# Factorization machine on one core: the remainders of V are computed on GpSimd instead of VectorE

## The reference

```python
B, VOCAB, F = (512, 6250, 64)
xf = x.astype(V.dtype)                      # x: int32, 0 or 1
xv = xf @ V                                 # V: 6250 x 64 float32
sum_sq = jnp.sum(xv * xv, axis=-1)
sq_sum = xf @ jnp.sum(V * V, axis=-1)
second_order = 0.5 * (sum_sq - sq_sum)
linear = g_bias + xf @ bias
return linear + second_order[:, None]       # 512 x 1
```

## Time and profile before

| | before |
|---|---|
| time, median of 3 runs (lowest, highest) | 48.98 us (48.85, 49.02) |
| profiled execution: its own time | 49.03 us |
| profiled execution: span | 47.2 us |
| mean granted TensorE clock in it | 0.996 of full |
| busy: DVE, PE, POOL, ACT | 30.5, 22.0, 20.5, 13.7 us |

### The profile page before, as it was taken

How to read it: one execution, slowest core, us unless ns; L and a number is a source line. 1 busy time by engine, 2 the same in 40 slices (tenths; PEclk the granted TensorE clock), 3 DMA queues, 4 the chain that set the end, 5 groups by cost and what they waited for, 6 DMA issues and landing times.

```text
span 47.2 us, 634 instructions
## 1 busy us (share of the span) xinstructions
PE 22.0 (46%) x210; PEld 20.1 (43%) x210; DVE 30.5 (65%) x74; ACT 13.7 (29%) x30; POOL 20.5 (43%) x34
## 2 busy tenths in 40 slices
PE   0000000000000000045999995999999999997200
PEld 0000000000000000045989893998999899985100
DVE  2000000000999469997999899999999999998600
ACT  0000009100899469954996300020002000000000
POOL 1999800000199009999599999990000000000000
PEclk9999999999999999999999999999999999999998
DMA  0399999999999999999999999999999970000000
GB/s 0 102 152 100 109 140 152 164 189 158 175 174 172 181 170 178 146 142 108 105 106 106 106 106 106 101 104 103 116 96 101 94 55 3 0 0 0 0 2 0
DMA packets 5583, 4.87 MB, mean 103 GB/s; under 512 B 1434, under 2 KB 5581, under 8 KB 5581
## 3 DMA queue, kind: packets, MB, share of 16 engines
q0 software_dynamic: 3456, 3.21, 73.4%
q1 hardware_dynamic: 1155, 0.82, 6.7%
q10 hardware_dynamic: 970, 0.81, 5.3%
HBM read 14.48 MB, written 0.00 MB: 307 GB/s over the span
## 4 chain that ended last, share of the span: by engine, by line
DVE 42%; DMA 34%; ACTq 10%; issue 4%; PE 2%; ACT 1%
DMA v_in<-in_L_rec_V_dram 34%; DVE x_all L330 13%; DVE seen L344 13%; ACTq L150 5%; DVE v_rest L295 3%; ACTq L237 3%; DVE xv L354 3%; DVE w_sum L301 2%; DVE xv_sq L359 2%; DVE odd_turned L335 2%; PE xv_ps L466 2%; ACTq L233 2%; DVE seen L406 1%; ACTq L234 1%; DVE seen L350 1%
## 5 line engine op out<-in xcount | busy, mean ns | idle before, releaser
L466 PE MATMUL xv_ps<-wall,x_all 128*128 128x195 bf16 x192 | 19.9, 266 | 1.8 <-DVE x_all L330 1.8
L466 PEld LDWEIGHTS xv_ps<-wall,x_all 128*128 128x128 fp8e4 x192 | 18.0, 105 | 2.7 <-DVE x_all L330 1.1
L160 POOL DMA_DIRECT2D x_all<-in_r_x_dram x24 | 13.0, 551 | 0.8 <-POOLq L498 0.8
L216 POOL TENSOR_TENSOR wall<-v_rest 128x512 bf16<-128x512 f32 (+1 forms) x6 | 7.4, 1247 | 10.2 <-DVE v_rest L295 10.2
L450 PE MATMUL g_ps<-g_in,ones 1*128 1x1 f32 x2 | 0.6, 342 | 20.2 <-DMA g_in<-in_L_rec_g_bias_dram 20.2
L450 PEld LDWEIGHTS g_ps<-g_in,ones 1*128 1x128 f32 x2 | 0.5, 305 | 20.2 <-issue 20.2
L330 DVE STREAM_TRANSPOSE x_all<-x_all 128x512 uint32<-128x512 uint32 (+1 forms) x13 | 8.5, 652 | 0.0
L364 DVE MEMSET v_in<- 22x64 f32 x1 | 0.1, 112 | 10.6 <-DMA v_in<-in_L_rec_V_dram 10.6
L344 DVE TENSOR_TENSOR seen<-seen,x_all 128x512 uint32<-128x512 uint32 (+1 forms) x10 | 6.3, 628 | 0.0
L251 ACT ACTIVATE v_sq<-v_in 128x512 f32<-128x512 f32 (+1 forms) x6 | 3.8, 636 | 5.3 <-DVE v_in L364 3.5
L295 DVE TENSOR_TENSOR v_rest<-v_in 128x512 f32<-128x512 f32 (+1 forms) x6 | 4.3, 750 | 1.4 <-DMA v_in<-in_L_rec_V_dram 1.3
(11 more groups left out here) (27 smaller groups left out, 9.5 us busy)
## 6 DMA issues: line engine op xcount, KB each, us to landing
x_all<-in_r_x_dram POOLq DMA_DIRECT2D x12, 196.0 KB, 9.7
v_in<-in_L_rec_V_dram ACTq DMA_DIRECT2D x6, 128.0 KB, 13.3
v_in<-in_L_rec_V_dram SPq DMA_DIRECT2D x6, 128.0 KB, 11.3
x_all<-in_r_x_dram POOLq DMA_DIRECT2D x4, 100.0 KB, 7.4
x_all<-in_r_x_dram POOLq DMA_DIRECT2D x4, 64.0 KB, 8.5
x_all<-in_r_x_dram POOLq DMA_DIRECT2D x4, 32.0 KB, 8.1
bias_in<-in_L_rec_bias_dram ACTq DMA_DIRECT2D x3, 6.5 KB
v_in<-in_L_rec_V_dram SPq DMA_DIRECT2D x1, 24.0 KB
```

What stands on the lines that cost most here:

```text
L160: queue.dma_start(x_words[S * i:S * i + S, t, :, lo // QUAD:hi // QUAD].bitcast(fp8), rows[:, :, START[i] + lo:START[i] + hi]).then_inc(x_ ...
L216: nc.gpsimd.tensor_tensor(placed(n, 2), v_part(v_rest, n), upper(v_rest, n), ALU.subtract).then_inc(low_placed, 1)
L466: last = nc.tensor.matmul(xv_ps[t][:, :, :], rows[:, q, :], wall[:, 1 + QUAD * d + q, :, 0:E], start=(d + q == 0), stop=(d == ND - 1 and q ...
```

## The change

The function `keep_rest` leaves DVE's program. Its two waits and its subtraction stand now at the head of POOL's `place_low(n)`, so that POOL makes the remainder of half n and then, after a wait for that remainder, the low part of half n. The order of the loads on POOL's queue and the order of everything else on every engine stay as they are.

```diff
         @block.gpsimd
         def _(pool):
             def place_low(n):
+                pool.wait_ge(v_landed[n // 2], V_COUNT[n // 2])
+                if n == 0:
+                    pool.wait_ge(overlap_cleared, 1)
+                nc.gpsimd.tensor_tensor(v_part(v_rest, n), v_part(v_in, n), upper(v_in, n), ALU.subtract
+                                        ).then_inc(rest_ready, 1)
                 pool.wait_ge(rest_ready, n + 1)
                 nc.gpsimd.tensor_tensor(placed(n, 2), v_part(v_rest, n), upper(v_rest, n), ALU.subtract
                                         ).then_inc(low_placed, 1)
...
-            def keep_rest(n):
-                dve.wait_ge(v_landed[n // 2], V_COUNT[n // 2])
-                if n == 0:
-                    dve.wait_ge(overlap_cleared, 1)
-                nc.vector.tensor_tensor(v_part(v_rest, n), v_part(v_in, n), upper(v_in, n), ALU.subtract
-                                        ).then_inc(rest_ready, 1)
...
             nc.vector.memset(v_in[last_quarter:last_quarter + OVER, 0, :], 0.0).then_inc(overlap_cleared, 1)
-            keep_rest(0)
-            keep_rest(1)
...
             weigh(0)
-            keep_rest(2)
-            keep_rest(3)
             sum_squares(2)
             sum_squares(3)
             weigh(1)
             turn(0)
-            keep_rest(4)
-            keep_rest(5)
             turn(1)
```

## The result

The changed kernel is slower. Four executions beside four of the kernel before gave medians of 51.61 us (50.86 to 52.37) and 49.00 us: a ratio of 1.043 (95% interval 1.032 to 1.054). All ratios leave out executions that took over 1.5% more than the fastest of their kernel, so they can differ from the quotient of the medians. Two executions of it were profiled: the first took 51.85 us with a span of 50.1, the second 50.80 with a span of 49.0. The kernel before's took 49.03 and, once more, 49.29.

What follows compares the result with a forecast made beforehand. The chain ending last, V's third load, then DVE with ACT, was taken to bound the kernel; POOL's queue would start turn_odd(0) at 27.85 instead of 26.20, so 49.03 + 1.65 = 50.68, stated as 50.7 us, range 50.1 to 52.8.

Steps and rivals of the forecast that it cites:

- The forecast shift: turn_odd(0) on DVE starts at 27.85 instead of 26.20, and the unchanged tail carries the whole 1.65 us to the end.
- V's landing: V's second load, from which POOL's chain was summed, was taken to land at 16.98 us, as in the one profile.
- Price of POOL's subtractions: Each remainder or low part on POOL costs 1.05 us for 512 elements, 1.18 for 576, plus 0.08 per wait.
- Rivals 1 and 2: POOL's waits cost a full start (52.3 us, chance 0.2); remainders cost POOL 1.42 us against 1.05 (52.5 us, chance 0.17).
- Hold-up between the engines: DVE and POOL delay each other when both have two inputs, worth 0.38 us for POOL; no large DVE subtraction remains.
- The step that ends w 2: DVE's sums 4 and 5 and w 2 end near 26.3, hidden before ACT's middle part 5, 1 us to spare.
- a sign of being wrong: The forecast is wrong if POOL holds up DVE's small steps of w beyond ACT's copies; no cost was added.
- x for t = 3 at no cost: POOL issues these loads 2.6 us later, at 27.95; the DMA backlog hides it; fully late would cost 0.4 us.
- rival 3: After a new gap before PE's third turn, 28 matmuls run at the slow pace: 1.1 us more, 51.8 us, chance 0.08.
- the 1.60 us: Remainders 4 and 5, from 21.92, are the only removed DVE subtractions on the chain; kept only if nothing else is late.

Runs made afterwards that it cites:

- after_again: The changed kernel measured once more in a later session, nothing altered: 51.36 us, ratio to the kernel before 1.042.
- before_early_x: The kernel before with the load of x for t = 2 issued right behind the first two x loads: 49.16 us, ratio 0.995.
- after_reordered_2: The program of after_reordered run again: four executions of 48.39 to 48.74 us (ratio to the kernel before 0.985), two of 49.86 and 50.02.
- both_rests: The changed kernel with VectorE also making all six remainders, into a spare tile nobody reads: 53.52 us, ratio to the kernel before 1.078.
- rests_first: The changed kernel with GpSimd's order altered, remainders ahead of low parts: 51.98 us, ratio to the kernel before 1.034.
- after_early_x: The changed kernel with the load of x for t = 2 issued right behind the first two x loads: 49.55 us, ratio to the kernel before 1.003.
- after_reordered: The changed kernel with x for t = 2 loaded early and x's first cast and turns moved into idle time: 48.22, 48.80 and four of 49.64 to 50.19 us.
- before_reordered: The kernel before with x for t = 2 loaded early and x's first cast and turns moved into idle time: 48.59 us, ratio 0.984.

## Why the prediction was right, and where it was not

- **Direction and size.** 50.7 was forecast with a range to 52.8; 51.6 and 51.4 were measured. The forecast shift was 1.65 us. Between the profiles of the later session it is 50.80 - 49.29 = 1.5; by the ratios of both sessions it is 2.1 (0.042 x 49.0 to 49.3). The rest, 0.4 to 0.6 us, stands in executions that were not profiled; V's landing and PE's clock, below, are the candidates, and which of them it is is not shown. So the mechanism was right, and that the total came so close is in part luck.
- **Price of POOL's subtractions.** 1.05 us taken for 512 elements; measured 1.042 and 1.047 (means of five remainders and five low parts of 512 elements, after_again), 1.14 and 1.15 for 576 (1.18 taken), 0.07 to 0.08 for each wait on itself. Rivals 1 and 2 both fall on these rows. The ratio of the Trainium skill (GPSIMD Engine Reference, Performance versus the Vector engine: 1.96, measured at 2048 elements) does not carry over to 512: here it is 1.04 to 0.69, 1.5.
- **Hold-up between the engines.** Read rightly for POOL, and then used on one side only. The step that ends w 2 "near 26.3, before ACT is through middle part 5: hidden, with 1 us to spare" priced its small operations as in the kernel before. They have two SBUF inputs as well, and in w 2 one of the three waited for the end of a subtraction of POOL in the first profile (0.90 us instead of 0.18) and two in after_again, where the chain above shows 1.09 and 0.95. These are the subtractions of POOL that they ended with:

```profile
25.85 1.04 POOL L218 TENSOR_TENSOR v_rest<-v_in 128x512 f32<-128x512 f32 x1
26.97 1.08 POOL L221 TENSOR_TENSOR wall<-v_rest 128x512 bf16<-128x512 f32 x1
```

In the first profile DVE still had 0.80 us of idle time before turn_odd(0), where 1.5 was forecast. In after_again it had none: w's last operation ends at 28.13, and turn_odd(0) starts at 28.00 with no wait for the cast at all. It cost nothing only because ACT's route ended at the same moment; that was luck, since the prediction had named this hold-up as a sign of being wrong and priced it at nothing. The Trainium skill has the rule (same page, section Key points: GpSimd shares its SBUF interfaces with VectorE, with contention when VectorE has two SBUF inputs); the runs agree, and add how long: until GpSimd has a gap.

- **A sign that was in the trace before.** The prediction took w's operations at 0.2 us. In the trace of the kernel before, one of w 1 took 1.04, and in after_again another took 0.92:

```profile
19.50 1.04 DVE L312 SCALAR_TENSOR_TENSOR w_all<-w_sum,bias_turned 128x16 f32<-128x16 f32 x1
```

```profile
19.93 0.92 DVE L315 TENSOR_TENSOR w_rest<-w_all 128x16 f32<-128x16 f32 x1
```

No subtraction ran beside these. Low 2 was over at 19.17 and at 19.49, and POOL was issuing the load of x for t = 2, from 19.12 and from 19.43; both operations ended 1.42 us behind that start. In before_early_x, with this load out of the way, the operation of w 1 took 0.71 us and ended with POOL's low parts. So something in issuing DMAs can hold VectorE up too. What it is stays open: VectorE's checks, also with two inputs, ran beside POOL's later issues at 0.65 to 0.69 us, as fast as without them.

- **x for t = 3 at no cost.** Right. Its DMAs were issued from 27.99 in after_again instead of 25.36, and the last cast ran at 35.44 (above), no later than the 36.25 of before. The backlog took up the delay, as the DMA issues show by their median from issue to landing, the last number (after_again, then the kernel before):

```profile
x_all<-in_r_x_dram POOLq DMA_DIRECT2D x4, 100.0 KB, 5.1
```

```profile
x_all<-in_r_x_dram POOLq DMA_DIRECT2D x4, 100.0 KB, 7.4
```

- **V's landing.** The sum hung on 16.98, from one profile. In the second profiles of the two kernels it is 17.2 to 17.3, and in the first of the changed kernel 18.3. That is the 1.2 us by which the first profile lies above the forecast.
- **PE's clock, rival 3.** Given 0.08 and counted as a case by itself. Of eight executions of the changed kernel, four have a mean granted clock of 0.932 to 0.966; no execution of the kernel before whose clock is on record is under 0.978. Three with 0.964 to 0.966 took 51.30 to 51.43 and the one with 0.932 took 52.37; the other four, from 50.80 to 51.85, differ by their landings at least as much. The two profiles that could be read are of the other four, so that this is the same fall of the clock as in after_reordered_2 is likely and not shown. The profiles of both_rests (idle time of 1.45 us before the third turn, then 0.50) and after_reordered_2 show the fall after such a gap; the two of the changed kernel, with 1.29 and 1.36 us of idle time, kept 1.00, and so did rests_first with 1.37 and 1.42. So the length of the gap alone does not decide it, and what does is not shown. The slow pace at 0.9 or more of the clock that rival 3 feared did not return: in after_again the 16 matmuls at 28.95 took 1.56 us, 0.098 each.

Where the 1.60 us went that left DVE's chain: DVE has it as idle time, since it waits for squares from ACT, which stood at middle part 3, and then gives 1.6 us back in w's waits (after_again; 0.7 in the first profile). With the queue put right (after_early_x) the changed kernel is level with the one before, and 0.8% behind the one before with the same order of loads. With DVE's idle time used as well, the remainders on GpSimd give 0.985 in the executions whose clock holds and those on VectorE give 0.984 in all. So in the best case the move buys nothing, and in half the executions of after_reordered it cost 1.2 us. before_reordered is the version to keep.

## What to carry to other kernels

An engine that runs in order is priced by its queue: before moving work to it, list what stands between the landing of the data and the last result that somebody waits for, issues of DMAs included, and ask whether these can go ahead of the first wait. In these runs, work moved from VectorE to GpSimd also held up what stayed on VectorE with two SBUF inputs, down to operations of 16 elements (0.7 to 1.1 us instead of 0.18). And where a chain comes to hang on another load, time it in more than one profile, since the landing varies, and look at the gaps that it opens on TensorE: in two profiles here the clock fell after one.

## What the runs showed that was not expected

- GpSimd's subtractions back to back leave VectorE's two-input operations no opening: 2.92 us for 16 elements (rests_first). A gap of 0.08 us, which a wait of GpSimd for its own result makes, is enough to let one in.
- Used in that way, a superfluous wait made a kernel faster by more than 1 us.
- The time of this kernel spreads with the landing of the first loads: V's second load came at 17.0 us in one profile and at 18.3 in another, though both kernels issue its DMAs in the same order.
